# Softmax attention on Trainium2: P times V over fifteen slots, and one fp32 unit made from two parts

## The chip, the cores and the metric

The kernel runs on one core of one Trainium2 chip. The metric is the device time in microseconds (us); the kernel before was run three times, and the median counts.

## The reference

The input is one sequence of 4096 tokens of width 256. Cut to what matters:

```python
x = layernorm(x + linear_attention(x))        # exp feature maps, width 64
h = layernorm(x) * g + b
q, k, v = (h @ W for W in (Wq, Wk, Wv))       # 16 heads of width 16
attn = softmax(q @ k.T / sqrt(16))            # 4096 x 4096 a head
x1 = x + (attn @ v) @ Wo
out = layernorm(x + x1 + moe(layernorm(x1)))  # top 2 of 8 experts
```

All of it is fp32. The change lies wholly in the softmax attention, the function `softmax_attention`, and there in `attn @ v`.

## The kernel before

`softmax_attention` works through 16 heads times 8 chunks of 512 queries, 128 chunks in all. The 4096 keys of a head are cut into 16 units of 256 keys (two sides of 128 keys, k = 0 and 1). A chunk has 16 slots, t = 0 to 15, and each engine has its order of work written out by hand, with semaphores between.

TensorE (`chunk`, L707 and on) issues in slot t, in this order:

- `scores(t)` (L673): two matmuls, keys by queries, for unit t of the chunk, into one of two halves of `s_ps`. It waits until the exponential of unit t-2 has read that half.
- `max_pair(t)` (L665): two matmuls that give block 2t and 2t+1 of scores, queries by keys, for the chunk two ahead (LEAD = 2); only their maximum per query is wanted. Their blocks go round three PSUM banks, `m_ps`, so each waits until the block three before it has been read (`m_read`).
- a visit, if the slot has one (`values`, L690 and L696): P times V for the units of `VISITS[i]` at the slot `SLOTS[i]`. A slot of 16 or more lies in the next chunk, at that number less 16.
- in slot 11 `turn_o` (L705), which folds the finished output of the chunk before; it uses one of the three banks as well.

ScalarE computes the exponential of each unit from `s_ps` (L761). At the slots of `RELU_PAIRS` it first turns the pair's first block into its positive part (L748), and after slot 8 it copies the last chunk's output (L752).

VectorE (`chunk`, `pair`) takes the maxima: two reductions a slot (L795), or for a pair of `RELU_PAIRS` one fused operation (L789) over the second block and what ScalarE made of the first; this reads both blocks at once. In slots 0 to 3 it finishes the maximum of the chunk in four small steps (`finish_max`, L810 to L822), of which the second and third (L813, L817) read two operands in SBUF. In slot 11 it copies the folded output to SBUF (L803). The maxima go by SP's DMA into the rows that `scores` multiplies.

P times V in fp32 is done in one of two ways. A full unit (`FULL_UNITS`) is one fp32 matmul a side. For every other unit the exponential is taken as a bf16 high part (`high_view`, the upper halves of the fp32 words) and an f16 rest: `probs_low` = probs - high, made by GpSimd (POOL) in `split_probs` (L623), one operation of 128x1024 a unit; TensorE multiplies both by a V that is held in bf16 pieces, two matmuls a side. All add up in `o_ps`. The visit of a split unit waits for POOL, and ScalarE overwrites a unit's `probs` in the next chunk only when its visit has passed (`pv_done`).

```python
VISITS = ((0, 1), (3,), (2, 4), (6,), (5, 7), (9,), (8, 10), (12,), (11, 13), (15,), (14,))
SLOTS = (10, 12, 14, 15, 16, 18, 19, 20, 22, 23, 24)
```

So slots 1, 5, 9 and 13 have no visit, slot 11 has the turn, and the relu pairs are at 1, 4, 7, 10 and 14.

Of the kernel before, what the change touches and what calls it, by code (L numbers as in the profile page):

```python
# [8 lines left out]
F16 = mybir.dt.float16  # L9
# [6 lines left out]
P = 128  # L16
# [3 lines left out]
CHUNK = 512  # L20
# [27 lines left out]
UNITS = SIDE // P  # L48
# [8 lines left out]
Q_DMAS = 16 * 2 * len(Q_PARTS)  # L57
ROW_DMAS = 16 * 2 * MROWS * (P // SQ)

FULL_UNITS = (3, 6, 9, 12, 15)  # L60
POOL_UNITS = tuple(t for t in range(UNITS) if t not in FULL_UNITS)
VISITS = ((0, 1), (3,), (2, 4), (6,), (5, 7), (9,), (8, 10), (12,), (11, 13), (15,), (14,))
SLOTS = (10, 12, 14, 15, 16, 18, 19, 20, 22, 23, 24)
COPY_SLOT, TURN_SLOT = 8, 11
RELU_PAIRS = (1, 4, 7, 10, 14)
FINISH_SLOTS = (0, 1, 2, 3)
RING_BLOCKS = 2 * UNITS + 1
TURN_BLOCK = 2 * TURN_SLOT + 2
# [393 lines left out]
def softmax_attention(nc, dram, keep):  # L462

    with ExitStack() as ctx:
        def sb(name, shape, dt=F32):
            return ctx.enter_context(nc.sbuf_tensor(name, shape, dt))
# [4 lines left out]
        def sem(name):  # L471
            return ctx.enter_context(nc.semaphore(name))
# [9 lines left out]
        zeros = sb("zeros", [P, TILES, DH])  # L482
        gather = sb("gather", [P, P])
        probs = sb("probs", [P, UNITS, 2, CHUNK])
        probs_low = sb("probs_low", [P, len(POOL_UNITS), 2, CHUNK], F16)
        no_max = sb("no_max", [P, TPC])
        excess = sb("excess", [P, CHUNK])
        unit_max = sb("unit_max", [P, 2, TPC, 2 * KCH])
# [12 lines left out]
        head_in, q_in = sem("head_in"), sem("q_in")  # L501
        v_ready, v_chain = sem("v_ready"), sem("v_chain")
        s_done, exp_done, pv_done = sem("s_done"), sem("exp_done"), sem("pv_done")
        pool_low_done = sem("pool_low_done")
        m_done, m_read, excess_ready = sem("m_done"), sem("m_read"), sem("excess_ready")
        unit_set, tile_max_done, high_done, low_done, max_ready = (
            sem("unit_set"), sem("tile_max_done"), sem("high_done"), sem("max_low_done"), sem("max_ready"))
# [71 lines left out]
        @block.gpsimd  # L579
        def _(pool):  # L580
            ch = Chain(pool, v_chain)
            nc.gpsimd.memset(k_ring[:, :, :].bitcast(F32), 1.0).then_inc(ones_set, 1)  # L582
            nc.gpsimd.memset(v_parts[:, :, :, V_ONE:V_COLS], 0.0).then_inc(v_consts, 1)
            nc.gpsimd.memset(v_full[:, :, :, :, :], 0.0).then_inc(v_consts, 1)
            nc.gpsimd.memset(zeros[:, :, :], 0.0).then_inc(v_consts, 1)
            nc.gpsimd.memset(gather[:, :], 0.0).then_inc(v_consts, 1)
            pool.wait_ge(v_consts, 4)
            nc.gpsimd.memset(v_parts[:, :, :, V_ONE:V_ONE + 1], 1.0).then_inc(v_consts, 1)
            nc.gpsimd.memset(v_full[:, :, :, :, V_ONE:V_ONE + 1], 1.0).then_inc(v_consts, 1)
            starts = [k * V_COLS + DH * n for k in range(2) for n in range(PIECES)]  # L590
            nc.gpsimd.tensor_tensor(gather[:, 0:DH], ident[:, 0:DH], ident[:, DH:2 * DH], ALU.add).then_inc(gather_chain, 1)
            for n, r in enumerate(starts[2:]):
                pool.wait_ge(gather_chain, n + 1)
                nc.gpsimd.tensor_tensor(gather[:, 0:DH], gather[:, 0:DH], ident[:, r:r + DH], ALU.add).then_inc(gather_chain, 1)
            nc.gpsimd.tensor_tensor(gather[:, DH:O_COLS], ident[:, V_ONE:V_ONE + 1],
                                    ident[:, V_COLS + V_ONE:V_COLS + V_ONE + 1], ALU.add).then_inc(gather_chain, 1)
            pool.wait_ge(gather_chain, len(starts))
            pool.wait_ge(v_consts, 6)
            pool.sem_inc(gather_ready, 1)

            def split_v(h, par):

                high, mid, low = (v_parts[:, par, :, DH * n:DH * n + DH] for n in range(PIECES))
                ch.inc(nc.gpsimd.tensor_copy(v_here[:, :, :], v_all[:, :, ds(h * DH, DH)]))
                ch.wait()
                for n, t in enumerate(FULL_UNITS):
                    at = first_tile(t)
                    ch.inc(nc.gpsimd.tensor_tensor(v_full[:, par, n, :, 0:DH], v_here[:, at:at + 3:2, :], zeros[:, 0:2, :], ALU.add))
                ch.inc(nc.gpsimd.tensor_tensor(high, v_here[:, :, :], zeros[:, :, :], ALU.add))
                ch.wait()  # L610
                ch.inc(nc.gpsimd.tensor_tensor(v_rest[:, :, :], v_here[:, :, :], high, ALU.subtract))
                ch.wait()
                ch.inc(nc.gpsimd.tensor_tensor(mid, v_rest[:, :, :], zeros[:, :, :], ALU.add))
                ch.wait()
                ch.inc(nc.gpsimd.tensor_tensor(low, v_rest[:, :, :], mid, ALU.subtract))
                ch.wait()
                pool.sem_inc(v_ready, 1)

            def split_probs(i):

                for t in POOL_UNITS:
                    pool.wait_ge(exp_done, i * UNITS + (t + 1))
                    nc.gpsimd.tensor_tensor(probs_low[:, POOL_UNITS.index(t), :, :], probs[:, t, :, :],  # L623
                                            high_view[:, t, :, :, 1], ALU.subtract).then_inc(pool_low_done, 1)

            def split_chunks(lo, hi):
                with pool.Fori(lo, hi) as i:
                    split_probs(i)

            for h in range(2):  # L630
                split_v(h, h)
            split_chunks(0, CHUNKS + 1)
            with pool.Fori(0, HEADS // 2 - 1) as pair:
                ch.enter(pair, 2 * SPLIT_OPS)
                for par in range(2):
                    h = pair * 2 + par
                    pool.wait_ge(pv_done, (h + 1) * (CHUNKS * len(VISITS)))
                    pool.sem_inc(pool_passed, 1)
                    split_v(h + 2, par)
                    with pool.Fori(1, CHUNKS + 1) as qc:  # L640
                        split_probs(pool.snap((h + 1) * CHUNKS + qc))
                ch.leave(HEADS // 2 - 1)
            split_chunks((HEADS - 1) * CHUNKS + 1, RING)

        @block.tensor
        def _(pe):
# [30 lines left out]
            def values(it, c, visit):  # L677

                par, i = c % PAIR // CHUNKS, it * PAIR + c
                if visit == 0 and c > 0:  # L680
                    pe.wait_ge(o_copied, i)
                if visit == 0 and c % CHUNKS == 0:
                    pe.wait_ge(v_ready, it * 2 + (c // CHUNKS + 1))
                for t in VISITS[visit]:
                    if t in POOL_UNITS:
                        pe.wait_ge(pool_low_done, i * len(POOL_UNITS) + (POOL_UNITS.index(t) + 1))
                    first, final = t == VISITS[0][0], t == VISITS[-1][-1]
                    if t in FULL_UNITS:
                        for k in range(2):
                            last = nc.tensor.matmul(o_ps[V_COLS * k:V_COLS * k + V_COLS, :],  # L690
                                                    v_full[:, par, FULL_UNITS.index(t), k, :], probs[:, t, k, :],
                                                    start=False, stop=False)
                        continue
                    for n, part in enumerate((high_view[:, t, :, :, 1], probs_low[:, POOL_UNITS.index(t), :, :])):
                        for k in range(2):
                            last = nc.tensor.matmul(o_ps[V_COLS * k:V_COLS * k + V_COLS, :],  # L696
                                                    v_parts[:, par, first_tile(t) + 2 * k, :], part[:, k, :],
                                                    start=(first and n == 0), stop=(final and n == 1))
                last.then_inc(pv_done, 1)
# [76 lines left out]
        def _(dve):  # L776
# [45 lines left out]
                    nc.vector.transpose(max_turned[:, :, :].rearrange("p r n -> p (r n)"),  # L822
                                        max_parts[:, :, :].bitcast(F32).rearrange("p r n -> p (r n)")).then_inc(max_ready, 1)

            def chunk(n, b, ahead=True, finish=True, turn=True, stores=None):

                for t in range(UNITS):
                    if ahead:
                        pair(n, t, b, 1 if t == TURN_SLOT and not turn else 0)
                    if t == TURN_SLOT and turn:  # L830
                        if not ahead:
                            dve.wait_ge(m_read, n * RING_BLOCKS)
                            dve.sem_inc(m_read, TURN_BLOCK)
                        copy_ctx(n - LEAD, 1 - b, stores)
                        if not ahead:
                            dve.wait_ge(m_read, n * RING_BLOCKS + TURN_BLOCK + 1)
                            dve.sem_inc(m_read, RING_BLOCKS - 1 - TURN_BLOCK)
                    if finish and not ahead and t == FINISH_SLOTS[0]:
                        dve.wait_ge(rows_in, (RING - 1) * ROW_DMAS)
                    if finish and t in FINISH_SLOTS:  # L840
                        finish_max(n - 1, 1 - b, FINISH_SLOTS.index(t))

            chunk(0, 0, finish=False, turn=False)
            chunk(1, 1, turn=False)
            chunk(2, 0, turn=False)
            chunk(3, 1)
            chunk(4, 0)
# [3 lines left out]
                    chunk(dve.snap(it * 2 + b), b, stores=it + (b - 2))  # L851
            chunk(RING, 0, ahead=False, stores=RING // 2 - 2)
            chunk(RING + 1, 1, ahead=False, finish=False, stores=RING // 2 - 1)
            chunk(RING + 2, 0, ahead=False, finish=False, stores=RING // 2 - 1)

def row_statistics(nc, dve, ch, stats, mean_var, std, rstd, var_ready, std_ready, n):
# [850 lines left out]
```

## Time and profile before

| | |
|---|---|
| median of 3 runs | 4740.93 us (4733.44 to 4748.56) |
| the profiled execution | 4736.03 us |
| its span in the trace | 4734.2 us |
| mean granted TensorE clock | 0.92 |
| busy, share of the span: TensorE | 4110.2 us, 87% |
| GpSimd | 3356.3 us, 71% |
| VectorE | 2870.3 us, 61% |
| ScalarE | 2803.7 us, 59% |

The profiled execution lies 1.8 us above its span and 4.9 us below the median. A busy share is an average over stages with different limits; the attention runs from about 320 to 3856 us of the span.
### The profile page before, as it was taken

The numbers are of one execution on the slowest core, as the hardware profiler recorded it, in microseconds if no ns is written. First come the engines' busy times: TensorE is split into PE (matmuls) and PEld (weight loads), VectorE is DVE, ScalarE is ACT, GpSimd is POOL, SyncE is SP. The second block draws the span as 40 slices with busy tenths as digits, with TensorE's granted clock in tenths as the row PEclk, the third lists the DMA queues.
The fourth block names the chain that finished last, engine by engine and source line by source line (L and its number), as shares of the span: only waits on it lengthen the run. The fifth ranks groups of instructions, "written<-read, shape, count | busy, mean of one in ns | idle before, by whom it ended". The sixth has DMA issues, their size and how long they took to land. (4 is left out here: it accounts for less than half of the span.)

```text
span 4734.2 us, 80747 instructions
## 1 busy us (share of the span) xinstructions
PE 4110.2 (87%) x21172; PEld 1951.4 (41%) x21172; DVE 2870.3 (61%) x5778; ACT 2803.7 (59%) x3421; POOL 3356.3 (71%) x1877
## 2 busy tenths in 40 slices
PE   7569999999999999999999999999999983499991
PEld 4333333333333333333333333333333343499991
DVE  3447666667666666766766777667666644133335
ACT  1226766667666666666666777667666641255550
POOL 0017787777778777877777787778787764788875
PEclk8778999999999999999998999999999995799995
DMA  2331101010101010110101010101010024344433
GB/s 79 124 104 20 19 9 21 9 19 10 19 9 20 9 19 9 21 19 9 21 9 19 9 20 9 20 10 19 10 20 9 9 77 157 123 139 139 139 116 116
DMA packets 145755, 205.72 MB, mean 43 GB/s; under 512 B 43537, under 2 KB 108433, under 8 KB 140177
## 3 DMA queue, kind: packets, MB, share of 16 engines
q1 hardware_dynamic: 127072, 173.76, 13.5%
q0 software_dynamic: 6336, 16.79, 1.1%
q10 hardware_dynamic: 12144, 12.06, 0.7%
q8 instruction: 178, 2.92, 0.3%
q14 instruction: 25, 0.20, 0.0%
HBM read 134.59 MB, written 66.85 MB: 43 GB/s over the span
## 5 line engine op out<-in xcount | busy, mean ns | idle before, releaser
L623 POOL TENSOR_TENSOR probs_low<-probs 128x1024 f16<-128x1024 f32 x1408 | 2636.7, 1893 | 803.2 <-ACT probs L761 799.6
L761 ACT ACTIVATE probs<-s_ps 128x1024 f32<-128x1024 f32 x2048 | 2070.6, 1024 | 656.6 <-PE s_ps L673 652.6
L795 DVE TENSOR_REDUCE unit_max<-m_ps 128x1 f32<-128x512 f32 x2816 | 1799.6, 684 | 510.1 <-PE m_ps L665 483.5
L665 PE MATMUL m_ps<-k_ring,q_stage 48*128 48x512 f32 x3456 | 1134.3, 440 | 261.7 <-DVE unit_max L789 152.3
L673 PE MATMUL s_ps<-q_stage,k_ring 50*128 50x512 f32 x4096 | 1037.1, 488 | 15.5 <-issue 15.2
L673 PEld LDWEIGHTS s_ps<-q_stage,k_ring 50*128 50x128 f32 x4096 | 400.3, 189 | 1020.6 <-ACT probs L761 541.2
L665 PEld LDWEIGHTS m_ps<-k_ring,q_stage 48*128 48x128 f32 x3456 | 535.7, 195 | 623.0 <-DVE unit_max L789 318.1
L789 DVE CUSTOM_DVE_ANT_0 excess<-m_ps,excess 128x512 f32<-128x512 f32 x640 | 442.6, 692 | 571.6 <-ACT excess L748 559.0
L690 PE MATMUL o_ps<-probs,v_full 128*64 128x512 f32 x2560 | 735.7, 654 | 0.0
L748 ACT ACTIVATE excess<-m_ps 128x512 f32<-128x512 f32 x640 | 380.8, 595 | 449.9 <-PE m_ps L665 449.6
L696 PE MATMUL o_ps<-probs,v_parts 128*64 128x512 bf16 x2816 | 594.9, 419 | 0.5 <-ACT probs L761 0.3
L696 PE MATMUL o_ps<-probs_low,v_parts 128*64 128x512 f16 x2816 | 552.4, 389 | 0.0
L1537 DVE TENSOR_TENSOR hidden_low<-h_ps,hidden_high 128x512 fp32r<-128x512 f32 x184 | 127.2, 691 | 366.5 <-ACT hidden_high L1501 366.5
L696 PEld LDWEIGHTS o_ps<-probs,v_parts 128*64 128x64 bf16 x2816 | 160.4, 111 | 323.1 <-issue 226.8
L1497 ACT ACTIVATE h_ps<-h_ps,b_here 128x512 f32<-128x512 f32 x184 | 121.4, 660 | 255.7 <-PE h_ps L1434 255.7
L665 PE MATMUL m_ps<-kd_ring,q_stage 48*128 48x512 f32 x640 | 260.0, 406 | 1.6 <-DVE unit_max L795 1.5
L690 PEld LDWEIGHTS o_ps<-probs,v_full 128*64 128x64 f32 x2560 | 129.8, 138 | 203.4 <-issue 202.8
L582 POOL MEMSET k_ring<- 114x4096 f32 x1 | 3.5, 3516 | 294.1 <-POOLq L110 294.1
L1446 PE MATMUL y_ps<-w_low,hidden_high 128*128 128x256 f32 x736 | 208.9, 284 | 0.0
L1446 PE MATMUL y_ps<-w_high,hidden_high 128*128 128x256 f32 x736 | 207.4, 282 | 0.0
L1446 PE MATMUL y_ps<-w_high,hidden_low 128*128 128x256 f32 x736 | 206.3, 280 | 0.0
L696 PEld LDWEIGHTS o_ps<-probs_low,v_parts 128*64 128x64 bf16 x2816 | 164.4, 113 | 73.5 <-issue 11.5
(194 smaller groups left out, 3588.9 us busy)
## 6 DMA issues: line engine op xcount, KB each, us to landing
w_in<-in_W SPq DMA_DIRECT2D x46, 1024.0 KB, 4.9
q_stage<-max_turned SPq DMA_DIRECT2D x2048, 0.5 KB
q_stage<-qs_dram SPq DMA_DIRECT2D x768, 32.0 KB, 1.8
k_ring<-ks_dram SPq DMA_DIRECT2D x96, 128.0 KB, 4.3
slots_dram<-zero_rows SPq DMA_DIRECT2D x24, 512.0 KB, 6.5
rows_e<-slots_dram SPq DMA_DIRECT2D x24, 512.0 KB, 3.9
y_slots_dram<-y_out ACTq DMA_DIRECT2D x23, 512.0 KB, 4.2
qs_dram<-parts SPq DMA_DIRECT2D x16, 512.0 KB, 2.8
```

The source lines that it names most:

```text
L623: nc.gpsimd.tensor_tensor(probs_low[:, POOL_UNITS.index(t), :, :], probs[:, t, :, :], high_view[:, t, :, :, 1], ALU.subtract).then_inc(poo ...
L665: nc.tensor.matmul(m_ps[:, b % 3, :], q_stage[at:at + SROWS, col:col + P], ring[at:at + SROWS, par, key:key + CHUNK], start=True, stop=Tru ...
L673: last = nc.tensor.matmul(s_ps[:, t % 2, k, :], k_ring[at:at + AROWS, par, P * t:P * t + P], q_stage[at:at + AROWS, buf * CHUNK:buf * CHUN ...
L690: last = nc.tensor.matmul(o_ps[V_COLS * k:V_COLS * k + V_COLS, :], v_full[:, par, FULL_UNITS.index(t), k, :], probs[:, t, k, :], start=Fal ...
L696: last = nc.tensor.matmul(o_ps[V_COLS * k:V_COLS * k + V_COLS, :], v_parts[:, par, first_tile(t) + 2 * k, :], part[:, k, :], start=(first ...
L748: nc.scalar.activation(excess[:, :], m_ps[:, block_of(t, 0) % 3, :], ACT.Relu).then_inc(excess_ready, 1)
L761: nc.scalar.activation(probs[:, t, :, :], s_ps[:, t % 2, :, :], ACT.Exp).then_inc(exp_done, 1)
L789: nc.vector.tensor_tensor_reduce(excess[:, :], m_ps[:, block_of(t, 1) % 3, :], excess[:, :], 1.0, LEAST, ALU.add, ALU.max, unit_max[:, b, ...
L795: nc.vector.tensor_reduce(unit_max[:, b, qt, 2 * j + k:2 * j + k + 1], m_ps[:, block_of(t, k) % 3, :], AX.X, ALU.max).then_inc(m_read, 1 + ...
L1446: last = nc.tensor.matmul(y_ps[:, b, t // 2, D * (t % 2):D * (t % 2) + D], h[:, f % 4, cols], w[:, b, f, :], start=(f == 0 and n == 0 and ...
L1497: nc.scalar.activation(h_ps[:, f % 2, :], h_ps[:, f % 2, :], ACT.Gelu_apprx_tanh, bias=b1_here[:, b, f:f + 1]).then_inc(h_read, 1)
L1537: nc.vector.tensor_tensor(hidden_low[:, f % 4, :], h_ps[:, f % 2, :], hidden_high[:, f % 4, :].bitcast(F32), ALU.subtract).then_inc(low_do ...
```

## The change

Unit 12 is no longer a full unit; four are left. Fourteen visits take the place of eleven, in slots 10 and 12 to 24 (with the turn in slot 11, fifteen slots in a row), and the relu pairs move. The units whose low part is made by an engine other than TensorE are now `LOW_UNITS`, twelve of them: POOL makes eleven (12 is new among them, 10 is not), and VectorE makes unit 10's in two operations of 128x512, right behind the pairs of slots 12 and 15. As VectorE is two chunks ahead with its maxima, this is slot 12 and 15 of the same chunk that the other engines are in.

```diff
-FULL_UNITS = (3, 6, 9, 12, 15)
-POOL_UNITS = tuple(t for t in range(UNITS) if t not in FULL_UNITS)
-VISITS = ((0, 1), (3,), (2, 4), (6,), (5, 7), (9,), (8, 10), (12,), (11, 13), (15,), (14,))
-SLOTS = (10, 12, 14, 15, 16, 18, 19, 20, 22, 23, 24)
+FULL_UNITS = (3, 6, 9, 15)
+DVE_UNITS = (10,)
+LOW_UNITS = tuple(t for t in range(UNITS) if t not in FULL_UNITS)
+POOL_UNITS = tuple(t for t in LOW_UNITS if t not in DVE_UNITS)
+DVE_PLACES = {12: (10, 0), 15: (10, 1)}
+VISITS = ((0, 1), (3,), (2,), (4,), (6,), (5,), (7,), (9,), (8,), (10,), (11, 12), (13,), (14,), (15,))
+SLOTS = (10, 12, 13, 14, 15, 16, 17, 18, 19, 20, 21, 22, 23, 24)
-RELU_PAIRS = (1, 4, 7, 10, 14)
+RELU_PAIRS = (2, 5, 8, 12, 15)
...
-        probs_low = sb("probs_low", [P, len(POOL_UNITS), 2, CHUNK], F16)
+        probs_low = sb("probs_low", [P, len(LOW_UNITS), 2, CHUNK], F16)
...
+                    if t in DVE_UNITS:
+                        pe.wait_ge(dve_low_done, i * (2 * len(DVE_UNITS)) + 2 * (DVE_UNITS.index(t) + 1))
...
-                                                    start=False, stop=False)
+                                                    start=False, stop=final)
...
+            def low(i, t, k):
+
+                dve.wait_ge(exp_done, i * UNITS + (t + 1))
+                nc.vector.tensor_tensor(probs_low[:, LOW_UNITS.index(t), k, :], probs[:, t, k, :], high_view[:, t, k, :, 1],
+                                        ALU.subtract).then_inc(dve_low_done, 1)
...
+                    if current and t in DVE_PLACES:
+                        low(n - LEAD, *DVE_PLACES[t])
```

## Rows read from the trace of the kernel before

**Rows 1.** Groups of the page: busy us, mean ns; idle before, releaser.
```profile
L623 POOL TENSOR_TENSOR probs_low<-probs 128x1024 f16<-128x1024 f32 x1408 | 2636.7, 1893 | 803.2 <-ACT probs L761 799.6
L795 DVE TENSOR_REDUCE unit_max<-m_ps 128x1 f32<-128x512 f32 x2816 | 1799.6, 684 | 510.1 <-PE m_ps L665 483.5
```

**Rows 2.** Stretches: length, busy by engine, granted clock, DMA share, GB/s.
```profile
2766.31:2792.61 26.30, 24.49 (x133) 9.57 (x131) 18.95 (x38) 18.90 (x22) 20.61 (x12) 1.00 0.34 55
2010.40:2038.20 27.80, 25.97 (x132) 9.71 (x130) 18.47 (x37) 18.41 (x23) 20.61 (x12) 0.93 0.04 9
```

**Rows 3.** The output copies (L752): durations, first and last; the 125th, timeline.
```profile
L752 ACT ACTIVATE o_here<-o_ps x128: 592/598/600, 402.0 to 3855.1; 128x512 f32<-128x512 f32 x128
...
3800.97 0.60 ACT L752 ACTIVATE o_here<-o_ps 128x512 f32<-128x512 f32 x1 [0.18 <-PE o_ps L696]
```

**Rows 4.** Timeline, TensorE, slots 8 to 12: start us, length us, instruction, [idle before].
```profile
2765.75 0.41 PE L696 MATMUL o_ps<-probs,v_parts 128*64 128x512 bf16 x2
...
2766.31 0.50 PE L673 MATMUL s_ps<-q_stage,k_ring 50*128 50x512 f32 x2
...
2766.64 0.40 PE L665 MATMUL m_ps<-k_ring,q_stage 48*128 48x512 f32 x2
2766.88 0.40 PE L673 MATMUL s_ps<-q_stage,k_ring 50*128 50x512 f32 x2
...
2768.25 0.42 PE L696 MATMUL o_ps<-probs,v_parts 128*64 128x512 bf16 x2
...
2769.26 0.50 PE L673 MATMUL s_ps<-q_stage,k_ring 50*128 50x512 f32 x2
...
2769.92 1.12 PE L705 MATMUL m_ps<-o_here,gather 128*128 128x512 f32 x2
...
2770.98 0.50 PE L673 MATMUL s_ps<-q_stage,k_ring 50*128 50x512 f32 x2
...
2771.81 1.08 PE L690 MATMUL o_ps<-probs,v_full 128*64 128x512 f32 x4
...
2772.82 0.50 PE L673 MATMUL s_ps<-q_stage,k_ring 50*128 50x512 f32 x2
```

**Rows 5.** Timeline, all engines, the relu pair of slot 1 and slot 2.
```profile
2779.44 0.39 PE L665 MATMUL m_ps<-kd_ring,q_stage 48*128 48x512 f32 x1
...
2779.87 0.60 ACT L748 ACTIVATE excess<-m_ps 128x512 f32<-128x512 f32 x1 [0.79 <-PE m_ps L665]
...
2780.36 1.94 ACT L761 ACTIVATE probs<-s_ps 128x1024 f32<-128x1024 f32 x2
2780.74 0.69 DVE L789 CUSTOM_DVE_ANT_0 excess<-m_ps,excess 128x512 f32<-128x512 f32 x1 [1.15 <-ACT excess L748]
...
2781.36 0.16 DVE L813 SCALAR_TENSOR_TENSOR max_parts<-tile_max,no_max 128x4 fp32r<-128x4 f32 x1
2781.43 1.28 DVE L795 TENSOR_REDUCE unit_max<-m_ps 128x1 f32<-128x512 f32 x2
2781.46 3.74 POOL L623 TENSOR_TENSOR probs_low<-probs 128x1024 f16<-128x1024 f32 x2 [0.40 <-ACT probs L761]
2781.49 0.49 PE L665 MATMUL m_ps<-k_ring,q_stage 48*128 48x512 f32 x1 [1.18 <-DVE unit_max L789]
2781.91 1.08 PE L690 MATMUL o_ps<-probs,v_full 128*64 128x512 f32 x4
...
2782.63 0.74 DVE L817 SCALAR_TENSOR_TENSOR max_parts<-tile_max,max_parts 128x4 fp32r<-128x4 f32 x1
```

**Rows 6.** Timeline, POOL and VectorE meeting; last, all of L1393: ns min/median/max.
```profile
361.52 5.60 POOL L623 TENSOR_TENSOR probs_low<-probs 128x1024 f16<-128x1024 f32 x3 [41.80 <-ACT probs L761]
...
363.38 1.90 DVE L813 SCALAR_TENSOR_TENSOR max_parts<-tile_max,no_max 128x4 fp32r<-128x4 f32 x1
...
4178.68 1.21 DVE L1520 TENSOR_TENSOR m_low<-mT_e,m_high 128x1024 fp32r<-128x1024 f32 x1
4179.02 3.35 POOL L1393 TENSOR_TENSOR w_high<-w_in,zero 128x1024 fp32r<-128x1024 f32 x1 [2.93 <-PEq L1465]
...
L1393 POOL TENSOR_TENSOR w_high<-w_in,zero x44: 2473/2967/3537, 4084.5 to 4585.8; 128x1024 fp32r<-128x1024 f32 x44
```

More of the change, by code:

```diff
@@ L503, in softmax_attention @@
         s_done, exp_done, pv_done = sem("s_done"), sem("exp_done"), sem("pv_done")
-        pool_low_done = sem("pool_low_done")
+        pool_low_done, dve_low_done = sem("pool_low_done"), sem("dve_low_done")
         m_done, m_read, excess_ready = sem("m_done"), sem("m_read"), sem("excess_ready")
@@ L622, in split_probs @@
                     pool.wait_ge(exp_done, i * UNITS + (t + 1))
-                    nc.gpsimd.tensor_tensor(probs_low[:, POOL_UNITS.index(t), :, :], probs[:, t, :, :],
+                    nc.gpsimd.tensor_tensor(probs_low[:, LOW_UNITS.index(t), :, :], probs[:, t, :, :],
                                             high_view[:, t, :, :, 1], ALU.subtract).then_inc(pool_low_done, 1)
@@ L691, in values @@
                                                     v_full[:, par, FULL_UNITS.index(t), k, :], probs[:, t, k, :],
-                                                    start=False, stop=False)
+                                                    start=False, stop=final)
                         continue
-                    for n, part in enumerate((high_view[:, t, :, :, 1], probs_low[:, POOL_UNITS.index(t), :, :])):
+                    for n, part in enumerate((high_view[:, t, :, :, 1], probs_low[:, LOW_UNITS.index(t), :, :])):
                         for k in range(2):
@@ L823, in finish_max, with chunk @@
                                         max_parts[:, :, :].bitcast(F32).rearrange("p r n -> p (r n)")).then_inc(max_ready, 1)
-            def chunk(n, b, ahead=True, finish=True, turn=True, stores=None):
+            def low(i, t, k):
+                dve.wait_ge(exp_done, i * UNITS + (t + 1))
+                nc.vector.tensor_tensor(probs_low[:, LOW_UNITS.index(t), k, :], probs[:, t, k, :], high_view[:, t, k, :, 1],
+                                        ALU.subtract).then_inc(dve_low_done, 1)
+            def chunk(n, b, ahead=True, finish=True, turn=True, stores=None, current=True):
                 for t in range(UNITS):
@@ L841, in chunk @@
                         finish_max(n - 1, 1 - b, FINISH_SLOTS.index(t))
-            chunk(0, 0, finish=False, turn=False)
-            chunk(1, 1, turn=False)
+            chunk(0, 0, finish=False, turn=False, current=False)
+            chunk(1, 1, turn=False, current=False)
             chunk(2, 0, turn=False)
@@ L853, in _ @@
             chunk(RING + 1, 1, ahead=False, finish=False, stores=RING // 2 - 1)
-            chunk(RING + 2, 0, ahead=False, finish=False, stores=RING // 2 - 1)
+            chunk(RING + 2, 0, ahead=False, finish=False, stores=RING // 2 - 1, current=False)
 def row_statistics(nc, dve, ch, stats, mean_var, std, rstd, var_ready, std_ready, n):
```

## The prediction

> **What bounds the kernel now.** I read the page's groups first. [rows 1] shows the softmax attention as the bulk of the span: 1408 subtractions on GpSimd (POOL) and 2816 plain maximum reductions on VectorE (DVE). No engine is full there. The stretches come next [rows 2]: in one chunk at full clock, 26.30 us, TensorE is recorded busy 24.49, POOL 20.61, VectorE 18.95, ScalarE 18.90. The reader should see two chunk lengths: 26.30 at a granted clock of 1.00, and 27.80 at 0.93 (part of the chunk at 1.2 GHz in place of 2.4). The copies of the output [rows 3] give the mean: (3800.97 - 402.0) / 124 chunks = 27.41 us. So the clock dips cost 27.41 - 26.30 = 1.11 us a chunk on average.
>
> A recorded-busy TensorE is not a streaming one, so I go to the timeline [rows 4]. TensorE issues, per slot t, scores s(t), the maximum pair m(t), then a visit of P times V. Times from start to start: s to m 0.33 (2766.31 to 2766.64), and as much from m on to what follows (s to turn 0.66, 2769.26 to 2769.92); one split unit 0.56 (2765.75 to 2766.31); two 1.01 (2768.25 to 2769.26); one full fp32 unit 1.01 (2771.81 to 2772.82); the turn 1.06 (to 2770.98). Slot 12's visit comes 0.83 after its s, 0.16 late, because its banks come free a little late. In a slot without a visit the two kinds follow at 0.24 and the next s gains the same: 0.57, and the slot behind it is 0.10 shorter. This gives slots of 1.23 (one split unit), 1.68 (two, or a full one), 1.73 (turn).
>
> Before: four empty slots 2.28; four filled ones behind them 4 x 1.57 = 6.28; slot 8 at 1.23; turn 1.73; six at 1.68 = 10.08. Sum 21.6. The other 26.3 - 21.6 = 4.7 us are TensorE waiting for one of the three maximum banks: m(t)'s second block needs m(t-1)'s first one read. The largest is in [rows 5]: a ScalarE-assisted pair (RELU_PAIRS) starts at 2779.44; ScalarE's Relu 2779.87, VectorE's fused reduce 2780.74, the next block only at 2781.49, 2.05 later, because slot 1 has no visit to cover it. One such round costs max(0, 2.05 minus the slot's length), and 0.10 where the pair is split.
>
> **The change, part by part.**
> TensorE's order. Unit 12 goes from full to split: -0.45. Fourteen visits in place of eleven: one empty slot (9) is left. New sum: 0.57 + 1.57 + 1.73 + four full slots (12, 15, 2, 8) and one double (5) at 1.68 = 8.40, + eight singles (13, 14, 0, 1, 3, 4, 6, 7) at 1.23 = 9.84. Sum 22.1, so +0.5: three more switches outweigh the cheaper unit.
> Relu pairs move to 2, 5, 8, 12, 15, all under a visit of 1.01: each round then stalls 2.05 - 1.68 = 0.37, plus 0.10, against up to 1.6 now. This is the gain. If the rounds were hidden whole it would be 0.47 x 5 = 2.4 us a chunk more.
> POOL still does 11 units (12 in, 10 out), with 11 to 14 now in a row. FULL_UNITS of four saves POOL a 32-element operation per head: nothing, it has idle time. SP's row copies hang on VectorE's transpose, which comes about a slot later; they are needed only at the next chunk's scores, some eleven slots on; SP's stores and loads keep their order. Cost nothing; without that cover it would be what the transpose is late by, under 2 us a chunk. `pv_done` counts 14: each unit is still visited before its buffer's next exponential, and slot 8 ends with 1.01 in place of 0.56 ahead of ScalarE's copy, whose result is wanted at slot 10. Nothing.
>
> VectorE's two halves. Price of one: half of the 128x1024 operation with two SBUF inputs, 1.21 / 2 = 0.61 [rows 6], and 0.69 for a 512-element one [rows 5]; the f16 result is not shown. I take 0.68; the halves queue ahead of pairs 13 and 0, which TensorE's banks wait for. Their wait on the exponential of unit 10 is two slots old and free. The price of the operation is small; its wait is not.
>
> The wait. [rows 6]: at 361.52 POOL starts three subtractions 1.86 apart; VectorE's max_parts, four elements wide but with two SBUF inputs, comes at 363.38, right as the second begins, and takes 1.90 in place of 0.16. The other way: POOL's w_high starts at 4179.02 while VectorE's m_low runs to 4179.89, and takes 3.35, 0.87 more than the least, 2.473. In [rows 5] the one of 2782.63 ends with POOL's operation (2781.46 + 1.89 = 3.35, it ends 3.37). So the one who starts first holds off the other for its whole operation. The halves have two SBUF inputs (probs and its high view), and POOL is running most of the time.
>
> Who wins? Time from the Relu of pair 12, which is at m(12) + 0.43. VectorE is ready at +1.49 (2779.87 to 2781.36), POOL's unit 12 at +1.59 (to 2781.46): VectorE wins the first half by 0.10, as the max_parts of 2781.36 does, and releases POOL at 1.49 + 0.68 = 2.17. POOL is then behind: unit 14 starts at 2.17 + 2 x 1.86 = 5.88. TensorE's m(15) comes after m(12) by: 2.05 to the second block of 13, 0.42 to its visit, 0.56 + 0.33 to m(14), 0.33 + 0.56 + 0.33 to m(15): 4.58. The second half is ready at 4.58 + 1.49 = 6.07: 0.19 too late. It waits to 5.88 + 1.74 = 7.62 (1.74 is the 1.90 of [rows 6] less the operation's own 0.16). A longer half doesn't help: above 0.71 it delays pair 13's bank and m(15) with it.
>
> The Trainium skill, page "SBUF — State Buffer", section "SBUF: two separate sides", calls this an exclusive lock on a shared port pair. The same page's section "A bandwidth-pool intuition that's wrong (but worth ruling out)" gives some 115 ns from VectorE's end until the blocked side goes on; [rows 6] shows none (4179.89 + 2.473 = 4182.37 = 4179.02 + 3.35). By the page unit 14 would start 0.11 later and the margin be 0.08 in place of 0.19, still lost.
>
> Walking the chunk from s(11) = 0 with these intervals, a reduce 0.68 [rows 1] (0.61 to the next), a bank reused 0.06 after its read: s(12) 1.73, s(13) 3.57, s(14) 5.10, s(15) 6.36, s(0) 8.01, s(1) 9.70. Pair 0 starts behind the late half, at 10.73; m(1)'s second block at 11.47 in place of 10.04. s(2) 12.45, s(3) 14.14. The maximum's own two small operations, at slots 1 and 2, no longer fall in POOL's gap and wait for units 1 and 2, to 14.56 and 16.72: s(4) 16.26, s(5) 18.38, s(6) 20.2, s(7) 21.75, s(8) 22.98, s(9) 24.66, s(10) 25.6, s(11) 27.60. That is 22.1 and 5.5 of stalls: 1.52 in slot 1, 0.89 each in 3 and 4, 0.46 in 0, 0.43 in 10, 0.37 in 9, 0.9 in the rest.
>
> Clock. The dips follow stalls (the long one in slot 2 now), and a stall like it remains. Between none and one a chunk (1.5), with 1.11 now; 27.60 has another rhythm, and the stalls are shorter, so I take 0.45, an estimate. New mean 28.05, +0.64 on 27.41, x 124 = +79 us. Profiled execution 4736.0 (span 4734.2) + 79 = 4815; the median of the runs is 5 above the profiled one, so 4819.
>
> **Rivals.**
> A. The second half also wins (the margin of 0.19 is wrong: POOL starts a little later, or TensorE reaches slot 15 sooner). Then slot 1's 1.52 goes; slots 3 and 4 keep 0.94 and 0.76 of the maximum's own waits: 26.0, with 0.4 for the clock 26.4. -1.0 x 124 = -125: 4612; 4561 without dips. For: 0.19 over seven terms is thin. Against: the terms are steady, and 363.38 shows that a hundredth late is fully late.
> B. It wins in some chunks and loses in others: half and half is 27.2, -24 us: 4712, anything from 4630 to 4800.
> C. No lock for these operations: the small waits go too, 24.6, +0.4 clock: -2.4 x 124 = -299: 4437. Against it stands all of [rows 6].
> D. POOL takes unit 12 first (0.10 of margin). Then the first half waits 1.76 and the second finds POOL idle: one loss a chunk again, as forecast.
> E. The loss costs as forecast, but the dips vanish: 27.6, +0.2 x 124 = +24: 4760.
>
> **How the numbers follow.** Forecast with D and E 0.56; A 0.26; B 0.14; C 0.04. No change that this kernel's measurement could tell is +-0.3%, 14 us. Faster: A, C and under half of B, 0.35; same 0.08, from B and the low end of E; slower 0.57. The forecast's own range is 4760 to 4900 (dips from none to 1.1 a chunk). As A holds a quarter, the whole range starts at its 4560.
>
> **What would show it.** In the new trace the second half (slot 15) lasts about 2.2 us, the first 0.68, and POOL's unit 12 is recorded longer by some 0.6; TensorE's m(1) waits 1.4 for VectorE; the two small maximum operations last over 1 us. A full-clock chunk of 27.6 says the walk holds; 26.0 says A. Both halves at 0.68 with POOL undisturbed would say C. Wrong above all if the interval of 4.58 or POOL's 5.88 is off by 0.2.

## The result and the profile after

The changed kernel takes 4856.69 us (median of 4 runs, 4844.63 to 4863.76) beside 4744.75 for the kernel before: a ratio of 1.0235, 95% interval 1.0203 to 1.0268. It is slower, as forecast, by 112 us where 79 were predicted; 4819 was the predicted time and 4560 to 4900 the range. The profiled execution took 4844.63 us, its span is 4842.9.

First the groups and the output copies that answer to [rows 1] and [rows 3], with the new group of VectorE's halves and its fused reductions (columns as there; lines five to seven: ns min/median/max, then the first and last start; the last line is the 125th copy).

```profile
L626 POOL TENSOR_TENSOR probs_low<-probs 128x1024 f16<-128x1024 f32 x1408 | 2747.0, 1970 | 784.8 <-ACT probs L766 777.0
L800 DVE TENSOR_REDUCE unit_max<-m_ps 128x1 f32<-128x512 f32 x2816 | 1790.9, 681 | 277.7 <-PE m_ps L668 271.0
L833 DVE TENSOR_TENSOR probs_low<-probs 128x512 f16<-128x512 f32 x256 | 364.1, 1423 | 0.3 <-DVEq L848 0.3
L794 DVE CUSTOM_DVE_ANT_0 excess<-m_ps,excess 128x512 f32<-128x512 f32 x640 | 441.7, 690 | 451.9 <-ACT excess L753 447.8
...
L757 ACT ACTIVATE o_here<-o_ps x128: 597/603/606, 404.1 to 3953.7; 128x512 f32<-128x512 f32 x128
L818 DVE SCALAR_TENSOR_TENSOR max_parts<-tile_max,no_max x128: 153/1214/1641, 343.0 to 3908.7; 128x4 fp32r<-128x4 f32 x128
L822 DVE SCALAR_TENSOR_TENSOR max_parts<-tile_max,max_parts x128: 156/1678/1868, 344.2 to 3910.4; 128x4 fp32r<-128x4 f32 x128
...
3895.40 0.60 ACT L757 ACTIVATE o_here<-o_ps 128x512 f32<-128x512 f32 x1
```

The mean of a half is 1423 ns for work of 0.69 us, and a four-element operation takes 1.2 or 1.7 us in the median. VectorE's operations with at most one SBUF input, on L800 and L794, keep their 0.68 and 0.69 beside the same POOL operations. The chunk is (3895.40 - 404.05) / 124 = 28.16 us, against 27.41 before: 0.75 x 124 = 93 us of the profiled execution's 109. Of the rest 4 us are in the last three chunks (58.3 against 54.2 us) and 12 in what lies before the first copy and behind the last.

The stretches of three chunks (columns of [rows 2]):

```profile
3731.30:3758.81 27.51, 25.77 (x133) 9.96 (x130) 23.26 (x40) 19.11 (x23) 21.53 (x12) 1.00 0.04 9
...
3786.76:3814.09 27.33, 26.33 (x134) 10.18 (x130) 21.83 (x40) 19.11 (x23) 21.53 (x12) 0.94 0.04 10
...
2693.31:2720.80 27.49, 26.56 (x133) 10.17 (x130) 23.26 (x40) 19.11 (x23) 21.54 (x12) 0.94 0.04 9
...
2720.80:2750.64 29.84, 28.93 (x133) 10.61 (x130) 23.30 (x40) 19.11 (x23) 21.59 (x12) 0.83 0.03 9
```

A chunk at full clock is 27.51 (26.30 before). Only 3 of the 124 chunks are at full clock now. Another 79 have a short stretch of 1.2 GHz in them (granted clock 0.94) and are no longer for it, 27.1 to 27.6. The other 42 are 28.2 to 32.3 us, most of them at 0.79 to 0.89; all that the mean lies above 27.51 comes from these. The experiment "POOL yields to the small operations" comes back to this.

The timeline of the full-clock chunk, from slot 12 on (columns of [rows 4]; POOL's starts are each read from a narrow window, so its lines overlap):

```profile
3737.81 0.69 DVE L833 TENSOR_TENSOR probs_low<-probs 128x512 f16<-128x512 f32 x1
3737.91 4.19 POOL L626 TENSOR_TENSOR probs_low<-probs 128x1024 f16<-128x1024 f32 x2 [0.47 <-ACT probs L766]
3740.21 3.74 POOL L626 TENSOR_TENSOR probs_low<-probs 128x1024 f16<-128x1024 f32 x2
3740.93 0.60 ACT L753 ACTIVATE excess<-m_ps 128x512 f32<-128x512 f32 x1 [0.35 <-PE m_ps L668]
3742.06 4.19 POOL L626 TENSOR_TENSOR probs_low<-probs 128x1024 f16<-128x1024 f32 x2
3742.42 2.08 DVE L833 TENSOR_TENSOR probs_low<-probs 128x512 f16<-128x512 f32 x1
3743.88 0.40 PE L668 MATMUL m_ps<-k_ring,q_stage 48*128 48x512 f32 x1
3744.42 1.28 DVE L800 TENSOR_REDUCE unit_max<-m_ps 128x1 f32<-128x512 f32 x2
3745.16 0.50 PE L668 MATMUL m_ps<-k_ring,q_stage 48*128 48x512 f32 x1 [0.88 <-DVE unit_max L800]
3746.91 1.21 DVE L818 SCALAR_TENSOR_TENSOR max_parts<-tile_max,no_max 128x4 fp32r<-128x4 f32 x1
3748.50 1.89 POOL L626 TENSOR_TENSOR probs_low<-probs 128x1024 f16<-128x1024 f32 x1 [0.39 <-ACT probs L766]
3748.66 1.75 DVE L822 SCALAR_TENSOR_TENSOR max_parts<-tile_max,max_parts 128x4 fp32r<-128x4 f32 x1
3750.12 0.40 PE L668 MATMUL m_ps<-k_ring,q_stage 48*128 48x512 f32 x1
3751.06 0.49 PE L668 MATMUL m_ps<-k_ring,q_stage 48*128 48x512 f32 x1 [0.54 <-DVE unit_max L800]
```

The reader should see the two races. In slot 12 VectorE comes 0.10 before POOL (3737.81 and 3737.91), takes its 0.69, and POOL's unit 12 is held: unit 13 starts 2.30 later and not 1.86. In slot 15 POOL's unit 14 starts at 3742.06, VectorE's half at 3742.42, and takes 2.08. Behind it pair 0 waits, and m(1)'s second block comes 1.28 after its first. Then the two small operations lose as well (1.21 and 1.75), the second to a POOL operation that started 0.16 before it, and m(4)'s blocks are 0.94 apart. All 128 second halves take 1.9 us or more. In the whole trace 334 operations of VectorE start behind one of POOL's and are held, and each of them goes on 0.14 us before the end of that POOL record (0.135 to 0.145, taken as its end less its own length); none is held for a second one.

### The profile page after: what moved, and what is told of

Same layout as the page of the kernel before. It is cut to its first block and busy times, and to the rows that moved or that the text cites. A ratio compares the mean times of both kernels' runs of the same rounds, so it can differ in the third digit from the quotient of the medians.

```text
span 4842.9 us, 81221 instructions
## 1 busy us (share of the span) xinstructions
PE 4306.8 (89%) x21172; PEld 2003.3 (41%) x21172; DVE 3326.9 (69%) x6034; ACT 2828.4 (58%) x3421; POOL 3474.2 (72%) x1861
## 5 line engine op out<-in xcount | busy, mean ns | idle before, releaser
L626 POOL TENSOR_TENSOR probs_low<-probs 128x1024 f16<-128x1024 f32 x1408 | 2747.0, 1970 | 784.8 <-ACT probs L766 777.0
L800 DVE TENSOR_REDUCE unit_max<-m_ps 128x1 f32<-128x512 f32 x2816 | 1790.9, 681 | 277.7 <-PE m_ps L668 271.0
L668 PE MATMUL m_ps<-k_ring,q_stage 48*128 48x512 f32 x3456 | 1246.5, 458 | 163.2 <-DVE unit_max L800 121.3
L676 PE MATMUL s_ps<-q_stage,k_ring 50*128 50x512 f32 x4096 | 1110.1, 523 | 16.2 <-issue 16.2
L668 PEld LDWEIGHTS m_ps<-k_ring,q_stage 48*128 48x128 f32 x3456 | 589.1, 201 | 488.3 <-DVE unit_max L800 259.8
L794 DVE CUSTOM_DVE_ANT_0 excess<-m_ps,excess 128x512 f32<-128x512 f32 x640 | 441.7, 690 | 451.9 <-ACT excess L753 447.8
L701 PE MATMUL o_ps<-probs,v_parts 128*64 128x512 bf16 x3072 | 671.2, 434 | 3.8 <-POOL probs_low L626 3.7
L695 PE MATMUL o_ps<-probs,v_full 128*64 128x512 f32 x2048 | 641.0, 709 | 0.0
L701 PE MATMUL o_ps<-probs_low,v_parts 128*64 128x512 f16 x3072 | 625.6, 404 | 0.0
L833 DVE TENSOR_TENSOR probs_low<-probs 128x512 f16<-128x512 f32 x256 | 364.1, 1423 | 0.3 <-DVEq L848 0.3
L668 PE MATMUL m_ps<-kd_ring,q_stage 48*128 48x512 f32 x640 | 277.9, 434 | 2.4 <-DVE unit_max L800 2.2
L701 PEld LDWEIGHTS o_ps<-probs_low,v_parts 128*64 128x64 bf16 x3072 | 181.1, 114 | 31.7 <-issue 8.3
```

Source lines behind the costliest of these rows:

```text
L626: nc.gpsimd.tensor_tensor(probs_low[:, LOW_UNITS.index(t), :, :], probs[:, t, :, :], high_view[:, t, :, :, 1], ALU.subtract).then_inc(pool ...
L668: nc.tensor.matmul(m_ps[:, b % 3, :], q_stage[at:at + SROWS, col:col + P], ring[at:at + SROWS, par, key:key + CHUNK], start=True, stop=Tru ...
L676: last = nc.tensor.matmul(s_ps[:, t % 2, k, :], k_ring[at:at + AROWS, par, P * t:P * t + P], q_stage[at:at + AROWS, buf * CHUNK:buf * CHUN ...
L794: nc.vector.tensor_tensor_reduce(excess[:, :], m_ps[:, block_of(t, 1) % 3, :], excess[:, :], 1.0, LEAST, ALU.add, ALU.max, unit_max[:, b, ...
L800: nc.vector.tensor_reduce(unit_max[:, b, qt, 2 * j + k:2 * j + k + 1], m_ps[:, block_of(t, k) % 3, :], AX.X, ALU.max).then_inc(m_read, 1 + ...
L833: nc.vector.tensor_tensor(probs_low[:, LOW_UNITS.index(t), k, :], probs[:, t, k, :], high_view[:, t, k, :, 1], ALU.subtract).then_inc(dve_ ...
```

## The experiments

All are timed beside the kernel before; "full clock" is the length of a chunk whose stretch shows a granted clock of 1.00.

| kernel | median us | ratio, 95% interval | mean chunk | full clock |
|---|---|---|---|---|
| before | 4741 to 4748 | | 27.41 | 26.30 |
| changed | 4856.7 | 1.0235 (1.0203 to 1.0268) | 28.16 | 27.51 |
| POOL yields to the half | 4647.1 | 0.9809 (0.9785 to 0.9832) | 26.54 | 25.89 |
| no halves | 4723.1 | 0.9961 (0.9943 to 0.9979) | 27.31 | 26.33 |
| first half out | 4730.5 | 0.9979 (0.9966 to 0.9992) | 27.29 | 27.08 |
| order only | 4717.7 | 0.9951 (0.9932 to 0.9969) | 27.19 | 26.78 |
| yields to the small ones | 4765.4 | 1.0041 (1.0025 to 1.0058) | 27.48 | 26.19 |
| yields at all three | 4497.1 | 0.9472 (0.9445 to 0.9499) | 25.34 | 24.81 |
| order only, yields | 4522.5 | 0.9528 (0.9501 to 0.9556) | 25.60 | 25.26 |
| no halves, yields | 4469.2 | 0.9414 (0.9387 to 0.9440) | 25.15 | 24.83 |
| before, yields | 4740.1 | 0.9990 (0.9977 to 1.0002) | 27.44 | 26.30 |

**The second half's lost start.** One wait is added to the changed kernel:

```diff
                 for t in POOL_UNITS:
                     pool.wait_ge(exp_done, i * UNITS + (t + 1))
+                    if t == 14:
+                        pool.wait_ge(dve_low_done, i * 2 + 2)
```

> The changed kernel, with one wait more: POOL starts unit 14 only when VectorE's second half is done. Nothing is left out. Theory (the lost start in slot 15 is the cost): the second half takes 0.69 us in place of 2.08, TensorE's wait in slot 1 goes, a full-clock chunk falls from 27.31 to about 25.7, with some 0.4 for the clock 26.1 against 28.16, so about -250 us: 4600. Rival (VectorE's added work and the three added visits are the cost, whoever goes first): the time stays within 40 us of the changed kernel's, or grows, since POOL, the engine with the longest queue here, now idles half a us a chunk.

Measured: 4647, 210 us below the changed kernel with every operation still done. All halves as one group (ns min/median/max) and a stretch at full clock:

```profile
L835 DVE TENSOR_TENSOR probs_low<-probs x256: 685/689/2377, 384.5 to 3739.5; 128x512 f16<-128x512 f32 x128
...
2791.52:2817.41 25.89, 25.33 (x133) 9.99 (x130) 21.64 (x40) 19.10 (x23) 21.02 (x12) 1.00 0.04 10
```

The median half is 0.69 and the chunk 25.89: 1.6 us gone, where slot 1's stall was 1.52 in the prediction. The two small operations still wait (1.43 and 1.32 in the median). The rival falls: VectorE does the same work. It is 47 us above what was expected, 0.2 of it a chunk in the walk, the rest the clock.

**Without the halves.** `DVE_PLACES = {}`, TensorE's wait for them dropped; unit 10's low part is a constant zero.

> The changed kernel without VectorE's two halves: the low part of unit 10 is set to zero once and not made. Theory: the same as with the halves never waiting, as they lie in VectorE's slack behind relu pairs: 25.6 a chunk at full clock, within 60 us of the kernel in which POOL yields: 4560 to 4600. Rival (the halves' own work on VectorE is the cost): this one is about 250 us faster than the changed kernel and the one in which POOL yields is not.

Measured: 4723, and so 76 us slower than the kernel that makes the halves and yields. Neither side foresaw this. VectorE and, below it, POOL around slot 1, timeline, then a stretch at full clock:

```profile
2767.08 1.87 DVE L817 SCALAR_TENSOR_TENSOR max_parts<-tile_max,no_max 128x4 fp32r<-128x4 f32 x1
...
2769.48 1.32 DVE L821 SCALAR_TENSOR_TENSOR max_parts<-tile_max,max_parts 128x4 fp32r<-128x4 f32 x1
...
2761.33 9.45 POOL L627 TENSOR_TENSOR probs_low<-probs 128x1024 f16<-128x1024 f32 x5
...
2856.42:2882.75 26.33, 25.32 (x133) 9.76 (x130) 21.15 (x38) 19.10 (x23) 20.62 (x12) 1.00 0.04 10
```

POOL runs five operations in a row from 2761.33, and the small operation of slot 1 arrives 0.04 after the fourth has started: 1.87 us, a whole operation. With the halves and the yield it was 1.44 there. Taking VectorE's work away moved POOL's phase, and another operation lost more; the full-clock chunk is 26.33 against 25.89, and that 0.44 is the same length. That it is also the cause is borne out further down: with the small operations freed, the kernel without halves is as fast at full clock as the one with them.

**A dose.** Only the half of slot 12 is left out (`DVE_PLACES = {15: (10, 1)}`; one side of unit 10's low part stays zero), so that POOL reaches unit 14 sooner.

> The changed kernel without the first half only (slot 12); one side of unit 10's low part stays zero. Theory: POOL is no longer held in slot 12, so unit 14 starts some 0.5 us sooner and the second half waits that much less: it takes about 1.6 in place of 2.08, chunks are 0.4 to 0.5 shorter at full clock, 26.85, the time about 50 us less: 4800. Rival (VectorE's work): half of what leaving out both halves gives, about 125 us less.

Measured: of the halves that are left, 113 of 128 take 1.6 to 1.7 us, and the chunk at full clock is 27.08:

```profile
2924.51:2951.59 27.08, 25.89 (x133) 10.03 (x130) 22.31 (x39) 19.11 (x24) 21.00 (x12) 1.00 0.04 10
```

Both as worked out: the wait is what is left of POOL's operation, and 0.43 less of it is 0.43 less chunk. The time, 126 us less and not 50, is the number that the rival gave for VectorE's work, but not its rule: half of what leaving out both halves gives would be 67 us (4857 to 4723). At full clock only 0.43 x 124 = 53 us of it are there; most of the others go with the clock, granted 0.98 on average from 480 to 3500 us against 0.92 in the changed kernel.

**The order alone.** The kernel before with the new visits and relu pairs, five full units, no low part on VectorE.

> The kernel before with the change's order of visits and relu pairs alone: five full units, POOL makes the low parts of the same eleven as before, VectorE none (unit 12 is visited alone in slot 21, units 11 and 13 together in slot 22). Nothing is left out. Theory: the order is the change's gain and by itself beats the kernel before: TensorE's issue sum is 22.6 and the stalls about 3.5, so 26.1 at full clock against 26.3, and fewer clock dips: 26.5 on average against 27.41, about -110 us: 4635, between 4600 and 4740. Rival (the added visits cost more than they cover): slower than before, 4780 or more.

Measured: 4718, faster than before by 0.5%, a fifth of what was expected. Its full-clock chunk is 26.78, longer than the 26.30 of before: 100 of its first small operations take 1.9 us and 101 of the second ones 1.3, which were 0.16 and 0.74. What the order gains TensorE it loses in the two small operations; the 0.5% is fewer chunks with a dip (26 against 72).

```profile
L813 DVE SCALAR_TENSOR_TENSOR max_parts<-tile_max,no_max x128: 151/1868/1877, 343.4 to 3787.3; 128x4 fp32r<-128x4 f32 x128
L817 DVE SCALAR_TENSOR_TENSOR max_parts<-tile_max,max_parts x128: 156/1319/1868, 344.5 to 3787.5; 128x4 fp32r<-128x4 f32 x128
...
2718.17:2744.95 26.78, 25.79 (x133) 9.90 (x130) 21.14 (x38) 19.10 (x23) 20.63 (x12) 1.00 0.04 10
```

**POOL yields to the small operations.** Added to the changed kernel, without unit 14's wait; the last chunk, which has no such operations, goes without:

```diff
+                    if small and t == 0:
+                        pool.wait_ge(high_done, i + 2)
+                    if small and t == 1:
+                        pool.wait_ge(low_done, i + 2)
```

> The changed kernel; POOL starts unit 0 only when VectorE's small operation of slot 1 (the negated maximum's high part) is done, and unit 1 only after the one of slot 2. Unit 14 does not wait. Nothing is left out. Theory (every two-operand operation of VectorE that starts behind one of POOL's costs its wait): the two small ones take 0.16 us in place of 1.2 and 1.8, the second half still 2.1; chunks at full clock 26.1 to 26.3 against 27.31, time about 4700. Rival (the small ones are off the path, since the maximum is wanted eleven slots later): no change, 4857, or slower as POOL idles 2 us more.

Measured: 4765, 91 us faster, so the small ones are on the path; 65 us short of the expectation. The first takes 0.15 now. The second takes 0.16 in half of the chunks and about 0.65 in most others, because unit 0, which goes ahead of it, is then still running. Two stretches:

```profile
3095.65:3121.84 26.19, 25.28 (x133) 9.92 (x130) 21.18 (x40) 19.10 (x23) 20.24 (x12) 1.00 0.05 10
...
2901.35:2928.64 27.29, 26.38 (x133) 9.93 (x130) 21.36 (x40) 19.10 (x23) 21.02 (x12) 0.94 0.04 9
```

The full-clock chunk is the expected 26.2, 1.3 below the changed kernel's, but 113 of 124 chunks have a dip, and most of them are 27.3. So a dip to 0.94 costs 1.1 here. In the changed kernel the same dip costs nothing. In 41 of its 79 such chunks the second small operation starts after POOL has finished and takes 0.16; they are 27.3 in the median. In 36 it waits its 1.76 as before, and they are 27.5, as long as at full clock. So freeing the small operation is worth 0.2, but it is not why the dip is free. Those dips lie where the two small operations hold TensorE up; that this hides them is an argument, which no run here tests.

**All three.**

> The changed kernel with POOL yielding at all three places: units 14, 0 and 1. Nothing is left out. Theory: no operation of VectorE waits for POOL; the walk without waits gives 24.6 a chunk, and the kernel that yields for the second half came 0.2 above its walk, so 24.8, with 0.4 for the clock 25.2 against 26.54 there: about 4480, faster than every kernel so far. Rival (POOL, 11 operations of 1.86 and two halves of 0.7 it stands still for, is the bound once it idles on purpose): chunks stay above 25.7, time above 4600.

Measured: 4497.1, and 4499.5 (ratio 0.9479, 0.9451 to 0.9507) when run once more, for which this was expected:

> The kernel that yields at all three places once more, beside the fourth corner on one chip: 4497, within 15 us.

The slots 12 to 1, all of the second small operations, and a stretch:

```profile
2699.81 0.69 DVE L840 TENSOR_TENSOR probs_low<-probs 128x512 f16<-128x512 f32 x1
2699.92 4.18 POOL L632 TENSOR_TENSOR probs_low<-probs 128x1024 f16<-128x1024 f32 x2 [0.47 <-ACT probs L773]
...
2704.42 0.69 DVE L840 TENSOR_TENSOR probs_low<-probs 128x512 f16<-128x512 f32 x1
2705.02 1.28 DVE L807 TENSOR_REDUCE unit_max<-m_ps 128x1 f32<-128x512 f32 x2
2705.18 1.89 POOL L632 TENSOR_TENSOR probs_low<-probs 128x1024 f16<-128x1024 f32 x1 [1.08 <-DVE probs_low L840]
...
2707.52 0.15 DVE L825 SCALAR_TENSOR_TENSOR max_parts<-tile_max,no_max 128x4 fp32r<-128x4 f32 x1
2707.75 1.89 POOL L632 TENSOR_TENSOR probs_low<-probs 128x1024 f16<-128x1024 f32 x1 [0.67 <-DVE max_parts L825]
...
L829 DVE SCALAR_TENSOR_TENSOR max_parts<-tile_max,max_parts x128: 157/639/1460, 343.7 to 3563.0; 128x4 fp32r<-128x4 f32 x128
...
2693.33:2718.14 24.81, 24.78 (x133) 9.81 (x130) 19.79 (x40) 19.10 (x23) 21.03 (x12) 1.00 0.05 10
```

POOL stands idle for 1.08 and 0.67 us on purpose, and the chunk is 24.81, the walk's 24.6 for no waits plus the 0.2 that it was known to be short. One wait is left: the second small operation starts while unit 0 runs and takes 0.64. This is the fastest of the versions that leave nothing out, 5.3% below the kernel before and 7.4% below the changed one. That POOL would become the bound is refuted.

**The order with the yields, and no halves with the yields.** POOL yields to the two small operations; the second kernel is the changed one with unit 10's low part a constant zero.

> The kernel before with the change's order alone, and POOL yielding to the two small operations (units 0 and 1). Nothing is left out; VectorE makes no low part. Theory: the order alone had its small operations waiting 1.9 and 1.3 us; without that its full-clock chunk falls from 26.8 to about 25.0, time about 4495; it is a little slower than the one that yields at all three places, by the 0.45 us that a full unit costs TensorE more than a split one, some 30 to 50 us. Rival: no change from 4718.

> The changed kernel without VectorE's two halves (unit 10's low part set to zero once), and POOL yielding to the two small operations. Theory: the halves' own work hides behind the relu pairs, so this is within 40 us of the kernel that yields at all three places, about 4460 to 4480. Rival (two operations of 0.69 a chunk on VectorE cost their time): this one is 1.2 us a chunk, about 150 us, faster than that.

Measured: 4522.5 and 4469.2. Two neighbouring chunks of the order with five full units, then two of the kernel with no halves:

```profile
2708.59:2733.85 25.26, 25.21 (x133) 9.70 (x130) 18.85 (x38) 19.11 (x23) 20.43 (x12) 1.00 0.05 10
2733.85:2759.20 25.35, 25.26 (x133) 9.62 (x130) 18.84 (x38) 19.10 (x23) 20.63 (x12) 1.00 0.04 10
...
2673.55:2698.38 24.83, 24.78 (x133) 9.58 (x130) 18.84 (x38) 19.11 (x23) 20.45 (x12) 1.00 0.05 10
2698.38:2723.31 24.93, 24.84 (x133) 9.56 (x130) 18.84 (x38) 19.10 (x23) 20.65 (x12) 1.00 0.05 10
```

Both have two lengths in turn, 25.26 and 25.35, and 24.83 and 24.91; the table has the shorter. With the halves it is 24.81: VectorE's 1.4 us of extra work a chunk costs nothing at full clock when it does not have to wait. The 28 us between 4469 and 4497 are elsewhere. About 5 are in the last three chunks. Nearly all the others are in eight stretches from output copy to output copy at changes of heads (the ninth, the 25th and so on), which are 27.6 to 31.6 us with the halves and 25.2 without. There POOL has just prepared another head's V and is behind. A unit earlier than 14 is still running when the second half starts, and the half takes 2.1 in spite of the yield. Five full units in place of four cost 0.44 (25.3 against 24.9 in the mean of the two lengths, neither with halves): the 0.45 that the visits' rows give for a split unit in place of a full one. Of the 251 us by which the kernel that yields at all three places beats the one before (4748.4 to 4497.1), moving the unit is worth 25, and not 0.45 x 124 = 56, because of those eight stretches and the last three chunks. The order with the yields was expected at about 4495 with chunks of 25.0, and is 27 us above that.

**The fourth corner.**

> The kernel before, its own order, with POOL's unit 1 started only when VectorE's small operation of slot 2 is done. Nothing is left out. This is the fourth corner beside the kernel before, its order changed alone, and both. Theory (VectorE's waits cost only where a bank is wanted next; in the order of before, the 0.58 us wait of slot 2 ends before pair 3 is ready, VectorE being idle 0.32 us behind it): the small operation falls from 0.74 to 0.16 us and the time stays within 20 us of before, 4730 to 4765. Rival (a wait for POOL costs its length wherever it stands): 0.58 x 124, about 70 us faster, 4675.

Measured: 4740.1, ratio 0.9990, the second small operation now 0.15; the first had nothing to wait for (0.16 in the kernel before), so only unit 1 yields. So in the order of before, VectorE's wait of 0.58 costs nothing. The rival, 70 us less, falls. It is a shorter wait than the two of the new order, though. The order alone gives 0.5%, the yields alone nothing, both together 4.7% (4522.5).

## Why the prediction was right

The mechanism was right, and its lengths come out of the trace. That the time lies in the range of 4560 to 4900 says less: the range is 7% wide and holds rivals A, B and E too.

- TensorE's issue sum (+0.5) and its gain from covered relu rounds. Borne out as a total by the walk without waits, 24.6 against 24.8 measured, though one wait of 0.5 was left there, and by the 0.44 between five full units and four.
- The first half wins by 0.10: it does, 3737.81 to 3737.91, and 118 of 128 take 0.69. Rival D (POOL first) came about only in the 9 that take 1.7.
- The second half loses. It lasts 2.08 in the normal chunk, 2.2 was predicted. The interval between the two Relus, 4.58 in the walk, is 4.61 (3740.93 against 3737.81 - 1.49). POOL's unit 14 came at 5.74 after the first and not 5.88, so the margin was 0.36 and not 0.19: a queued POOL goes on some 0.14 before the end of the record of VectorE's operation, as VectorE in [rows 6] gets through before POOL's. The Trainium skill, page "SBUF — State Buffer", section "A bandwidth-pool intuition that's wrong (but worth ruling out)", has some 115 ns after VectorE's end, measured with the writing of DMA descriptors. The trace does not agree for POOL's subtraction, which goes on 0.14 before that end. My reading of [rows 6] as "none" stood on the least of 44 durations, 2.473, where the median is 2.967, and could not tell a tenth. As VectorE lost with all 128 second halves, rivals A and B are refuted, and A had less behind it than 0.26.
- The small operations. Predicted to wait in slots 1 and 2, to 1.3 and 1.6; measured 1.21 and 1.75. The full-clock chunk is 27.51, the walk gave 27.60.
- The clock is the term that was mis-sized. I took 0.45 a chunk for it and said from none to 1.1. Measured on the mean chunk it is 28.16 - 27.51 = 0.65, but this hides more: the granted clock from 480 to 3500 us is 0.92 against 0.96 before, 79 of the dips cost nothing and 42 chunks carry it all. My reason, that the stalls are shorter now and so dips fewer, was wrong: 121 of 124 chunks have a dip, and 72 had one before. Nor is the difference between mean and full-clock chunk the clock alone: some 0.3 of it, now and before, lies in the chunks at changes of heads, and some of those are long at full clock too (27.6 for 24.8 once in the kernel that yields at all three places). The three lines of the changed kernel, "yields to the small ones" and "first half out" (0.92, 0.94, 0.98) show no rule that I could have used: the dips come and go with small shifts of phase.
- Of the miss of 38 us on the median, 0.11 x 124 = 14 is the chunk's mean (28.16 for 28.05); the rest is outside the term that was worked out: 4 in the last three chunks, where VectorE's order changes too and which I had not walked, 12 before the first copy and behind the last, and 8 because the median lies 12 above the profiled execution and not 4. (The prediction's 4815 and its 5 make 4820, not 4819.)
- Rivals C and E: C (no lock) is refuted by every line with 2.08 in it; E (the dips vanish) by the clock of 0.92.

What the prediction missed in kind is that rival A's experiment was within reach: one wait on POOL made it true and turned a loss of 2.4% into a gain of 1.9%.

## What to carry to other kernels

When VectorE gets an operation with two SBUF inputs while GpSimd runs long ones that read SBUF, as here, and starts behind one of them, its price is the rest of GpSimd's operation, not its own length: find in the trace which of them starts first, to the tenth of a microsecond, and settle it with a semaphore rather than leave it to phase. Make the engine with slack yield, for the small operations too, and look at where it is behind: a yield before one unit does not help against the unit before it. Before taking work off an engine, ask what its new phase will collide with: here less work was slower (4723 against 4647).

## What was not expected

- A VectorE operation on four elements a partition costs up to 1.9 us, a whole GpSimd operation, in 100 of 128 chunks of the order alone.
- A short dip of TensorE's clock to 1.2 GHz (granted clock 0.94) made 79 chunks of the changed kernel no longer: 27.1 to 27.6 us with one, 27.5 without. Longer or later ones did: 42 chunks are 28.2 us and more.
- Removing a stall can be eaten by the clock: 27.51 to 26.19 at full clock became 28.16 to 27.48 on average. Once few stalls were left, with all three yields, the clock took little: 25.34 on average, 24.81 at full clock, nearly all of the difference at the changes of heads.
